# A recurrent layer with a feed-forward beside it: state parts laid out by step, and feed-forward products moved behind the candidate's

## The chip, the core and the metric

The kernel runs on one core of a Trainium2 chip. The metric is the device time of one execution, in microseconds (us). A core has a matrix engine (TensorE, PE in the profile, with its weight loads as PEld), VectorE (DVE), ScalarE (ACT), GpSimd (POOL) and SyncE (SP), each with an instruction stream of its own, and they meet through semaphores.

## What is computed

The first of four layers is a gated recurrent unit over 512 steps for 4 sequences of width 256. A token-wise feed-forward with a hidden width of 1024 follows it, and its output replaces that of the recurrence at selected tokens. Then come a dense layer with experts chosen per sequence, and a layer of 64 experts. Only the first two matter here:

```python
def step(h, xs):
    xzt, xrt, xht = xs
    z = jax.nn.sigmoid(xzt + h @ U_z + vz)
    r = jax.nn.sigmoid(xrt + h @ U_r + vr)
    hh = jnp.tanh(xht + r * h @ U + vh)
    h_new = (1.0 - z) * h + z * hh
    return (h_new, h_new)
...
hidden = jax.nn.gelu(jnp.einsum('bsd,dh->bsh', x, W1) + b1, approximate=False)
blk = jnp.einsum('bsh,hd->bsd', hidden, W2) + b2
```

## The kernel before

**Numbers in parts.** The recurrence multiplies in f16 with every value split in two, a high part and a low part. Each product of a 256-wide vector by a 256x256 matrix is 8 matmuls with the high part of the moving side and 4 with its low part (`recur`). Each has 4 moving columns, one for each sequence.

**One step of the recurrence.** TensorE runs this list for step j, in this order:

1. 12 products of the last step's update (`step_high`, `step_low`) into the reset gate, after which ScalarE takes the tanh of r (L471, `r_h<-bank`);
2. 12 products of the state (shown as `raw`, high then low) into the update gate z, which ScalarE reads at L473 and L474;
3. beside z: one input product for the next window (L772, f32, 160 columns), and in some steps one feed-forward product;
4. 12 products of the gated state (`rh_high`, `rh_low`) into the candidate, whose tanh ScalarE takes at L478 (`z_cand<-bank`);
5. 8 products of the kept part (`keep_part`, high) into the next step's reset gate, then feed-forward products, then the 4 low products of the kept part.

VectorE stands between these. L704 and L595 make the gated state's parts, L711 to L717 the kept part's, L721 and L595 the update's. L730 writes the state's high part into `h16`, L735 and L737 the full state, and L741 the state's low part into `h16`, reading the high part back.

**Windows.** The 512 steps are cut in windows of 40 (`SPAN`), the last of which (12, `FINAL`) has 32. In window w the recurrence runs over its steps. Beside it TensorE makes the input products of window w+1 (36 matmuls, one in each of steps 0 to 35) and the feed-forward of window w-1: 48 up products (L818, 160 moving columns from `h16`) and 48 down products (L833). ScalarE takes the gelu of a hidden tile (L414), VectorE splits it into parts (L660, L663), and ScalarE writes the block's output (L419) and clears its accumulator (L425). GpSimd copies 16 steps of state away at a time (L501).

**What sets the order.** Everything is written out by hand. `up_products` and `down_products` give, for each step jj of a window, which feed-forward products go beside z and which behind the kept part's high products. Steps 0 to 3, 6 to 9, 12 to 15 and 18 to 21 of a window have one up product beside z and two later (16 steps). Steps 16, 17 and 22 to 31 have two down products later, steps 32 to 39 have three. Tuples such as `GELU_AT`, `SPLIT_AT` and `BLOCK_AT` name the steps in which ScalarE and VectorE do their share, always behind the step's own work.

**Layout.** `h16` holds the state's parts as [part, window parity, k and sequence, step]. The 160 columns of an up product are one run. The 4 columns that a recurrent product reads, and the 8 values that L730 and L741 write, stand 40 values (80 bytes) apart.

Of the kernel before, what the change touches and what calls it, by code (L numbers as in the profile page):

```python
# [8 lines left out]
F16 = mybir.dt.float16  # L9
# [31 lines left out]
AHEAD = 2  # L41
EPS = float(np.finfo(np.float32).eps)
# [21 lines left out]
def program(nc, A, out):  # L64
    with ExitStack() as ctx:
# [74 lines left out]
        with ExitStack() as weights:  # L140
# [8 lines left out]
            h16_at, hid16_at, full_at, scale_at = 0, 2 * KD * B * SPAN, 2 * KD * B * SPAN + KH * B * SPAN, 2 * KD * B * SPAN + (KH + 2) * B * SPAN  # L149
            h16 = raw[:, h16_at:hid16_at].bitcast(F16).rearrange("p (x q c t) -> p x q c t", x=2, q=2, c=KD * B)  # L150
            hid16 = raw[:, hid16_at:full_at].bitcast(F16).rearrange("p (x u c) -> p x u c", x=2, u=KH)
            full16 = raw[:, full_at:scale_at].rearrange("p (u c) -> p u c", u=2)
# [3 lines left out]
            under = (w16_1, w16_2, h16, hid16, full16, blk, fsc, silu_c, b1, b2)  # L156
# [6 lines left out]
            last_q = LAST // SPAN % 2  # L163
            last_under = (w16_1, w16_2, lambda x, k: h16[:, x, last_q, k * B:(k + 1) * B, 0:tail],
                          [[hid16[:, x, u, 0:n_last] for u in range(KH)] for x in range(2)],
                          [full16[:, u, 0:n_last] for u in range(2)], blk, fsc, silu_c, b1, b2)
# [41 lines left out]
def gru(nc, sem, A, bank, xT, hist, ident, ones, ones_bf, condT, slot_row, s_x, s_const, load_ffn_up, load_ffn_down, load_next,  # L208
        up_loaded, down_loaded, shared_loaded, raw, shared_parts, under, ffn_sems, wr, wr_rep, idle_rows):

    with ExitStack() as own:
# [3 lines left out]
        w16_1, w16_2, h16, hid16, full16, blk, fsc, silu_c, b1, b2 = under  # L215
# [72 lines left out]
        HIGH_AT, LOW_AT = 3, (7, 8)  # L288
# [42 lines left out]
        FFN_HIGH_AT = ((0, 27), (0, 28), (0, 33), (0, 34), (0, 39), (1, 0), (1, 1), (1, 2))  # L331
# [5 lines left out]
        BLOCK_AT, CLEAR_AT, CLEAR_FINAL_AT = (1, 2), (33, 34), 5  # L337
        GELU_FINAL_AT = (3, 4, 6, 8, 12, 13, 18, 19)
        SPLIT_FINAL_AT = ((4, 5), (6, 7), (8, 9), (10, 11), (13, 14), (15, 16), (19, 20), (21, 22))
        BLOCK_FINAL_AT = (1, 2, 30, 31)  # L340

        def up_products(window, jj):
            if window == FINAL:
                if jj < 6:
                    return 4 * jj, 4 * jj + 2, 4 * jj + 4
                return (2 * jj + 12, 2 * jj + 14, 2 * jj + 14) if jj < 18 else (0, 0, 0)
            at = jj // TERMS * 2 * TERMS + jj % TERMS * 3
            return (at, at + 1, at + 3) if jj < 4 * TERMS and jj % TERMS < 4 else (0, 0, 0)

        def down_products(window, jj):  # L350
            if window == FINAL:
                return (2 * jj - 12, 2 * jj - 10) if 6 <= jj < 30 else (0, 0)
            if jj in (16, 17):
                return 2 * jj - 32, 2 * jj - 30
            if 22 <= jj < 32:
                return 2 * jj - 40, 2 * jj - 38
            return (3 * jj - 72, 3 * jj - 69) if jj >= 32 else (0, 0)

        with nc.Block() as block:
# [20 lines left out]
            def _(act):  # L380
# [27 lines left out]
                def gelu(F):  # L408
                    span, f = F // KH, F % KH
                    n = columns(span)  # L410
                    act.wait_ge(s_fup, F // 2 * 2 + 2)
                    if F >= 2:
                        act.wait_ge(s_flo, F - 1)
                    nc.scalar.activation(full16[:, F % 2, 0:n], up_columns(bank, f, n), ACT.Gelu,  # L414
                                         scale=fsc[:, 9:10], bias=b1[:, f:f + 1]).then_inc(s_gelu, 1)
# [1492 lines left out]
```

## Time and profile before

| what | us |
|---|---|
| median of 3 runs | 2192.7 |
| lowest and highest | 2191.93, 2192.86 |
| the profiled execution | 2195.69 |
| its span, first to last instruction | 2193.8 |
| mean granted TensorE clock | 0.995 of full speed |

The profile lists, for an engine or a line, the busy time, the mean duration of an instruction and what it waited for. A timeline row has the start in us, the busy time of the row, engine, line, operation, output and inputs, the shape and the count, and in brackets the idle time before it with who ended it. The ends of matmuls are modelled, so TensorE's pace is read from the distance between starts. The span falls in two parts: the recurrence with the feed-forward beside it (up to some 1100 us) and all that follows.

### The profile page before, as it was taken

What the parts mean: (1) busy time and instruction counts of PE and PEld (TensorE: products, weight loads), DVE (VectorE), ACT (ScalarE), POOL (GpSimd) and SP (SyncE); (2) the same over time, 40 slices, a digit from 0 to 9 for tenths busy, and PEclk for the clock granted to TensorE, in tenths of its full rate; (3) what the DMA queues carried; (4) which work ended last, traced back from release to release, by engine and by line L of the source; (5) the groups of instructions that cost most, each with busy time, mean ns of one, the idle gap of its engine ahead of it and who ended that gap; (6) DMA issues with size and microseconds to landing.
All of it is one profiled execution on the core that took longest, in us unless ns stands there. A gap on an engine that the chain in (4) does not pass through costs nothing. (4 is left out here: it accounts for less than half of the span.)

```text
span 2193.8 us, 83018 instructions
## 1 busy us (share of the span) xinstructions
PE 2136.1 (97%) x32790; PEld 2007.3 (91%) x32797; DVE 1603.0 (73%) x8952; ACT 1014.6 (46%) x3948; POOL 432.7 (20%) x593
## 2 busy tenths in 40 slices
PE   8999999999999999999979999999999999999997
PEld 7899999999999999999957888866999999999997
DVE  6887777877877877777845555494677777777775
ACT  3555555555555555555545767633222222222221
POOL 0000000000000000000000000254455555555553
PEclk9999999999999999999999999999999999999999
DMA  3001000000000000000000423211888888888882
GB/s 123 4 4 43 4 4 4 4 4 4 4 4 4 4 4 4 4 4 4 4 1 11 153 77 116 104 58 48 297 284 263 285 263 286 265 285 263 282 265 58
DMA packets 55559, 213.74 MB, mean 97 GB/s; under 512 B 11578, under 2 KB 40960, under 8 KB 46976
## 3 DMA queue, kind: packets, MB, share of 16 engines
q1 hardware_dynamic: 36276, 184.41, 22.9%
q0 software_dynamic: 17408, 23.61, 5.7%
q8 instruction: 258, 4.23, 0.8%
q14 instruction: 133, 1.09, 0.2%
q10 hardware_dynamic: 1484, 0.40, 0.1%
HBM read 192.82 MB, written 15.57 MB: 95 GB/s over the span
## 5 line engine op out<-in xcount | busy, mean ns | idle before, releaser
L1789 PE MATMUL bank<-xe,ring 128*128 128x160 f32 x3072 | 439.4, 300 | 0.7 <-DVE xe L1839 0.7
L1789 PEld LDWEIGHTS bank<-xe,ring 128*128 128x128 f32 x3072 | 423.7, 190 | 0.9 <-issue 0.9
L803 PE MATMUL bank<-keep_part,Us 128*128 128x4 f16 x6132 | 322.8, 170 | 0.8 <-DVE keep_part L711 0.4
L803 PEld LDWEIGHTS bank<-keep_part,Us 128*128 128x128 f16 x6132 | 306.1, 111 | 5.0 <-DVE keep_part L717 2.4
L1832 DVE STREAM_TRANSPOSE turned<-ye 32x64 f32<-32x64 f32 x1240 | 291.5, 235 | 16.2
L803 PE MATMUL bank<-raw,Us 128*128 128x4 f16 x6144 | 265.5, 170 | 2.3 <-DVE raw L741 1.7
L1817 ACT ACTIVATE gate_f<-bank 128x160 f32<-128x160 f32 x384 | 116.4, 303 | 288.1 <-PE bank L1789 280.5
L1744 POOL DMA_INDIRECT out_rows<-res,to_row x128 | 192.3, 1503 | 234.7 <-DVE res L1851 201.0
L803 PEld LDWEIGHTS bank<-raw,Us 128*128 128x128 f16 x6144 | 231.8, 104 | 3.0 <-DVE raw L741 2.5
L501 POOL TENSOR_TENSOR hist<-ring,unscale 128x128 f32<-128x128 f32 x32 | 17.0, 531 | 1081.4 <-DVE ring L735 1081.4
L471 ACT ACTIVATE r_h<-bank 128x8 f32<-128x8 f32 x512 | 92.8, 181 | 293.5 <-PE bank L803 293.5
L1798 PE MATMUL bank<-mid,ring 128*128 128x160 f32 x1536 | 220.1, 300 | 2.1 <-DVE mid L1860 2.1
L772 PE MATMUL bank<-in_part,W_part 128*128 128x160 f32 (+1 forms) x468 | 215.0, 474 | 0.0
L1798 PEld LDWEIGHTS bank<-mid,ring 128*128 128x128 f32 x1536 | 212.7, 190 | 2.4 <-DVE mid L1860 2.4
L803 PE MATMUL bank<-rh_high,Us 128*128 128x4 f16 x4096 | 205.9, 172 | 8.3 <-DVE rh_high L704 0.5
L1860 DVE TENSOR_TENSOR mid<-bank,gate_f 128x160 f32<-128x160 f32 x384 | 117.5, 317 | 130.8 <-ACT gate_f L1817 120.7
L803 PEld LDWEIGHTS bank<-rh_high,Us 128*128 128x128 f16 x4096 | 183.7, 113 | 24.2 <-DVE rh_high L704 18.3
L803 PE MATMUL bank<-step_high,Us 128*128 128x4 f16 x4096 | 190.2, 168 | 6.1 <-issue 0.8
L476 ACT ACTIVATE z_cand<-tz,lift 128x8 f32<-128x8 f32 x512 | 156.0, 305 | 16.5
L803 PEld LDWEIGHTS bank<-step_high,Us 128*128 128x128 f16 x4096 | 149.2, 105 | 14.3 <-DVE step_high L721 3.6
L721 DVE TENSOR_TENSOR step_high<-z_cand 128x8 f16<-128x8 f32 x512 | 89.4, 175 | 96.4 <-ACT z_cand L478 83.3
L818 PE MATMUL bank<-raw,ffn_parts 128*128 128x160 f16 x576 | 148.4, 330 | 0.0
(269 smaller groups left out, 4088.4 us busy)
## 6 DMA issues: line engine op xcount, KB each, us to landing
ring<-in_ew SPq DMA_DIRECT2D x64, 2304.0 KB
raw<-in_L_cond_ew SPq DMA_DIRECT2D x16, 1024.0 KB, 6.3
ctx_rows<-rows SPq DMA_DIRECT2D x2, 1280.0 KB, 6.7
dense_w<-in_L_ffn_W SPq DMA_DIRECT2D x2, 1024.0 KB, 9.4
dense_w<-in_L_cond_sw SPq DMA_DIRECT2D x2, 1024.0 KB, 6.3
out_rows<-orow SPq DMA_DIRECT2D x4, 512.0 KB, 3.9
out_rows<-res,to_row POOLq DMA_INDIRECT x128
xT<-in_xT SPq DMA_DIRECT2D x2, 864.0 KB, 10.4
```

Of the source, the lines that this page charges most:

```text
L471: nc.scalar.activation(r, pre_of(0, q, jj), ACT.Tanh, scale=inv[0]).then_inc(s_r, 1)
L476: nc.scalar.activation(z, tz[:], ACT.Identity, scale=2.0 ** (STATE_EXP - 1), bias=lift[:, 0:1]).then_inc(s_z, 1)
L721: nc.vector.tensor_tensor(step_high[:, :, 2], z, cand, ALU.mult).then_inc(s_shi, 1)
L772: last = nc.tensor.matmul(product(span, n), W_part[w][:, g, k, m * P:(m + 1) * P], steps_of(x_part[x], span)[:, k], start=(k == 0 and i == ...
L803: last = nc.tensor.matmul(pre[g][q][:, jj, m, :], Us[:, g, p, k, m * P:(m + 1) * P], x[part][:, k * B:(k + 1) * B], start=False, stop=Fals ...
L818: last = nc.tensor.matmul(up_columns(bank, f, columns(span)), w16_1[w][:, k, f * P:(f + 1) * P], h16[:, x, span % 2, k * B:(k + 1) * B, 0: ...
L1744: nc.gpsimd.indirect_dma_start(out=out[:, :], out_offset=bass.IndirectOffsetOnAxis(ap=to_idx[c][:, 0:1], axis=0), in_=res[e % 2][c][:], in ...
L1789: last = nc.tensor.matmul(bank[f % UPS][:, s_ * CAP:(s_ + 1) * CAP], w1[u][:, k, s_ * FFN + f * P:s_ * FFN + (f + 1) * P], xe[e % 2][:, k] ...
L1798: last = nc.tensor.matmul(bank[6 + e % 2][:, d * CAP:(d + 1) * CAP], w2[u][:, f, d * P:(d + 1) * P], mid[e % 2][:, f], start=(f == 0), sto ...
L1817: nc.scalar.activation(gate[:, f % 2], bank[f % UPS][:, CAP:2 * CAP], ACT.Silu).then_inc(s_silu, 1)
L1832: last = nc.vector.transpose(y[:, :, q, :], ye[e % 2][q * SQ:(q + 1) * SQ, :, j * SQ:(j + 1) * SQ])
L1860: nc.vector.tensor_tensor(mid[e % 2][:, f], bank[f % UPS][:, 0:CAP], gate[:, f % 2], ALU.mult).then_inc(s_mid, 1)
```

## The change

The layout: `h16` becomes `h_steps`, [part, window parity, step, k and sequence]. The 8 values of one step are one run, so L730 and L741 write one run and a recurrent product reads 4 adjacent values. The 160 columns of an up product are now 40 runs of 4 values (8 bytes) that start 16 bytes apart. The hidden tile's columns are therefore ordered by step and then sequence, and the block's output is read from the accumulator with a step of 4 values.

The order: no feed-forward product stands beside z, except in the final window. All come right behind the candidate's products and ahead of all of the kept part's.

```diff
-            h16 = raw[:, h16_at:hid16_at].bitcast(F16).rearrange("p (x q c t) -> p x q c t", x=2, q=2, c=KD * B)
+            h_steps = raw[:, steps_at:hid16_at].bitcast(F16).rearrange("p (x q t c) -> p x q t c", x=2, q=2, t=SPAN)
...
-        HIGH_AT, LOW_AT = 3, (7, 8)
+        HIGH_AT, LOW_AT = 4, (7, 8)
...
-        def h16_of(p, j):
+        def part_of(p, j):
             if j < 0:
-                return h16[:, p, 1, :, SPAN - 1]
-            return h16[:, p, j // SPAN % 2, :, j % SPAN]
+                return h_steps[:, p, 1, SPAN - 1]
+            return h_steps[:, p, j // SPAN % 2, j % SPAN]
...
-        SHARED_HIGH_AT = [(span, at) for span in range(3, 7) for at in (0, 4)]
-        SHARED_LOW_AT = [(span, at) for span in range(3, 7) for at in (1, 2, 3, 4, 5, 6, 9, 14)]
+        SHARED_HIGH_AT = [(span, SPAN - 1) for span in range(3, 11)]
+        SHARED_LOW_AT = [(span, at) for span in range(4, 12) for at in range(LOWS)]
...
+        UP = count([(0, 3, 3, 3, 3, 0)[jj] if jj < TERMS else (3, 3, 2, 2, 2, 0)[jj % TERMS] if jj < 4 * TERMS else 0 for jj in range(SPAN)])
+        DOWN = count([3 if jj in (17, 23) or 24 <= jj < 34 else 2 if jj >= 34 else 0 for jj in range(SPAN)])
+        UP_FINAL_BESIDE_Z = count([2 if 1 <= jj <= 16 else 0 for jj in range(TAIL)])
+        UP_FINAL_LATER = count([1 if 1 <= jj <= 16 else 0 for jj in range(TAIL)])
+        DOWN_FINAL_BESIDE_Z = count([2 if 17 <= jj < 24 else 0 for jj in range(TAIL)])
+        DOWN_FINAL_LATER = count([2 if 8 <= jj < 25 else 0 for jj in range(TAIL)])
...
-                                         block_columns(bank, span, d, columns(span)).rearrange("p (b t) -> p b t", b=B),
+                                         block_columns(bank, span, d, columns(span)).rearrange("p (t b) -> p b t", b=B),
...
-                                            h16[:, x, span % 2, k * B:(k + 1) * B, 0:LENGTHS[span]],
+                                            h_steps[:, x, span % 2, 0:LENGTHS[span], k * B:(k + 1) * B],
...
+                        if span:
+                            for n in later[0]:
+                                ffn_up(span, n)
+                            if later[1] and span < FINAL:
+                                pe.wait_ge(s_tz, m)
+                            for n in later[1]:
+                                ffn_down(span, n)
                         nq, njj = (q, jj + 1) if jj < LENGTHS[span] - 1 else (1 - q, 0)
                         if m < S:
                             if njj == 0:
                                 pe.wait_ge(s_seed, (span + 1) * GROUPS * B)
                             pe.wait_ge(s_khi, m)
                             recur(0, nq, njj, kept, 0)
-                        if span:
-                            for n in range(middle, end):
-                                ffn_up(span, n)
-                            if down_products(span, jj)[1]:
-                                pe.wait_ge(s_z, m)
-                            for n in range(*down_products(span, jj)):
-                                ffn_down(span, n)
-                        if m < S:
                             pe.wait_ge(s_klo, m)
                             recur(0, nq, njj, kept, 1)
```

The gelu's output gets 8 buffers in place of 2 (`FULLS`). The steps of some ScalarE and VectorE work shift: the block's output from steps 1 and 2 to 2 and 3, the split of the shared expert's weights (L687 and its high half) from windows 3 to 6 to the last and first four steps of windows 3 to 11, and those of the final window. The up products no longer wait for the seeding of the next window; the input products wait for the gelu that frees their bank from tile 2 on.

TensorE in step 6 of window 2, before, from the input product to the end of the step; `raw,ffn_parts` are feed-forward products:

```order
L772 MATMUL bank<-in_part,W_part 128x160
L818 MATMUL bank<-raw,ffn_parts 128x160 [waits ffn_hidden_done]
L803 MATMUL bank<-rh_high,Us 128x4 [waits rh_hi]
L803 MATMUL bank<-rh_high,Us 128x4 x7
L803 MATMUL bank<-rh_low,Us 128x4 [waits rh_lo]
L803 MATMUL bank<-rh_low,Us 128x4 x3
L803 MATMUL bank<-keep_part,Us 128x4 [waits keep_hi]
L803 MATMUL bank<-keep_part,Us 128x4 x7
L818 MATMUL bank<-raw,ffn_parts 128x160 x2
L803 MATMUL bank<-keep_part,Us 128x4 [waits keep_lo]
L803 MATMUL bank<-keep_part,Us 128x4 x3
```

The same place in the changed kernel:

```order
L784 MATMUL bank<-in_part,W_part 128x160
L815 MATMUL bank<-rh_high,Us 128x4 [waits rh_hi]
L815 MATMUL bank<-rh_high,Us 128x4 x7
L815 MATMUL bank<-rh_low,Us 128x4 [waits rh_lo]
L815 MATMUL bank<-rh_low,Us 128x4 x3
L828 MATMUL bank<-raw,ffn_parts 128x160 [waits ffn_hidden_done]
L828 MATMUL bank<-raw,ffn_parts 128x160 x2
L815 MATMUL bank<-keep_part,Us 128x4 [waits keep_hi]
L815 MATMUL bank<-keep_part,Us 128x4 x7
L815 MATMUL bank<-keep_part,Us 128x4 [waits keep_lo]
L815 MATMUL bank<-keep_part,Us 128x4 x3
```

The up product that stood ahead of the candidate's products now stands behind them with the two others, and the three stand ahead of the kept part's high products.

TensorE in step 24 of window 2, before, behind the gated state's low products:

```order
L803 MATMUL bank<-keep_part,Us 128x4 [waits keep_hi]
L803 MATMUL bank<-keep_part,Us 128x4 x7
L833 MATMUL bank<-raw,ffn_parts 128x160 [waits z_done]
L833 MATMUL bank<-raw,ffn_parts 128x160
L803 MATMUL bank<-keep_part,Us 128x4 [waits keep_lo]
L803 MATMUL bank<-keep_part,Us 128x4 x3
```

The same place in the changed kernel:

```order
L843 MATMUL bank<-raw,ffn_parts 128x160 [waits ffn_hidden_low,z_turned]
L843 MATMUL bank<-raw,ffn_parts 128x160 x2
L815 MATMUL bank<-keep_part,Us 128x4 [waits keep_hi]
L815 MATMUL bank<-keep_part,Us 128x4 x7
L815 MATMUL bank<-keep_part,Us 128x4 [waits keep_lo]
L815 MATMUL bank<-keep_part,Us 128x4 x3
```

Three down products stand there in place of two, ahead of the kept part's high products, and they wait for the tanh of z (L474) and no longer for z itself (L476).

## Rows read from the trace of the kernel before

**Rows 1.** Busy time of each engine in window 7: us, busy (instructions), clock, DMA.

```profile
core 0: us, PE busy (x) PEld busy (x) DVE busy (x) ACT busy (x) POOL busy (x), PEclk, DMA share, GB/s
614.20:698.20 84.00, 83.16 (x2056) 81.61 (x2054) 65.75 (x498) 46.88 (x237) 1.15 (x3) 1.00 0.02 4
```

**Rows 2.** ScalarE's timeline: tanh of r opening windows 7, 8, 12; second row step 1.

```profile
614.20 0.18 ACT L471 ACTIVATE r_h<-bank 128x8 f32<-128x8 f32 x1 [0.90 <-PE bank L803]
...
616.31 0.18 ACT L471 ACTIVATE r_h<-bank 128x8 f32<-128x8 f32 x1 [0.81 <-PE bank L803]
...
698.25 0.18 ACT L471 ACTIVATE r_h<-bank 128x8 f32<-128x8 f32 x1 [0.90 <-PE bank L803]
...
1035.65 0.18 ACT L471 ACTIVATE r_h<-bank 128x8 f32<-128x8 f32 x1 [0.90 <-PE bank L803]
```

**Rows 3.** Timeline of window 7, step 12 (one up product beside z).

```profile
639.76 0.18 ACT L471 ACTIVATE r_h<-bank 128x8 f32<-128x8 f32 x1 [0.57 <-PE bank L803]
...
639.96 0.48 PE L772 MATMUL bank<-in_part,W_part 128*128 128x160 f32 x1
...
640.25 0.36 PE L818 MATMUL bank<-raw,ffn_parts 128*128 128x160 f16 x1
...
640.39 0.40 PE L803 MATMUL bank<-rh_high,Us 128*128 128x4 f16 x8
...
640.94 0.18 ACT L478 ACTIVATE z_cand<-bank 128x8 f32<-128x8 f32 x1 [0.21 <-PE bank L803]
...
641.93 0.18 ACT L471 ACTIVATE r_h<-bank 128x8 f32<-128x8 f32 x1 [0.57 <-PE bank L803]
```

**Rows 4.** Timeline of window 7, step 26 (input product alone beside z).

```profile
669.59 0.18 ACT L471 ACTIVATE r_h<-bank 128x8 f32<-128x8 f32 x1 [0.57 <-PE bank L803]
...
669.80 0.48 PE L772 MATMUL bank<-in_part,W_part 128*128 128x160 f32 x1
...
670.08 0.42 PE L803 MATMUL bank<-rh_high,Us 128*128 128x4 f16 x8
...
670.64 0.18 ACT L478 ACTIVATE z_cand<-bank 128x8 f32<-128x8 f32 x1
...
671.46 0.20 DVE L741 SCALAR_TENSOR_TENSOR raw<-ring,raw 128x8 f16<-128x8 f32 x1
671.63 0.18 ACT L471 ACTIVATE r_h<-bank 128x8 f32<-128x8 f32 x1 [0.57 <-PE bank L803]
...
671.84 0.48 PE L772 MATMUL bank<-in_part,W_part 128*128 128x160 f32 x1
```

**Rows 5.** Timeline of window 12, step 5 (two up products, no input product).

```profile
1045.76 0.18 ACT L471 ACTIVATE r_h<-bank 128x8 f32<-128x8 f32 x1 [0.44 <-PE bank L803]
...
1045.96 0.43 PE L818 MATMUL bank<-raw,ffn_parts 128*128 128x160 f16 x2
...
1046.20 0.38 PE L803 MATMUL bank<-rh_high,Us 128*128 128x4 f16 x8
...
1047.74 0.18 ACT L471 ACTIVATE r_h<-bank 128x8 f32<-128x8 f32 x1 [0.39 <-PE bank L803]
```

**Rows 6.** Timeline of window 7, steps 32 and 33 (three down products later).

```profile
681.86 0.18 ACT L471 ACTIVATE r_h<-bank 128x8 f32<-128x8 f32 x1 [0.59 <-PE bank L803]
...
683.95 0.18 ACT L471 ACTIVATE r_h<-bank 128x8 f32<-128x8 f32 x1 [0.61 <-PE bank L803]
...
685.99 0.18 ACT L471 ACTIVATE r_h<-bank 128x8 f32<-128x8 f32 x1 [0.66 <-PE bank L803]
```

**Rows 7.** Two VectorE lines: duration of one, ns, min/median/max.

```profile
L741 DVE SCALAR_TENSOR_TENSOR raw<-ring,raw x512: 193/195/233, 24.3 to 1100.1; 128x8 f16<-128x8 f32 x171
...
L717 DVE TENSOR_TENSOR keep_part<-keep,keep_part x512: 166/167/169, 23.3 to 1099.4; 128x8 f16<-128x8 f32 x171
```

**Rows 8.** Groups of instructions by line and shape: busy us, mean ns, idle before.

```profile
L1044 PE MATMUL bank<-x_part,weights_part 128*128 128x512 f32 x576 | 136.8, 395 | 5.4 <-DVE x_part L1229 5.4
...
L419 ACT ACTIVATE ffn_out<-bank,b,raw 128x160 f32<-128x160 f32 x24 | 11.5, 478 | 0.0
```

More of the change, by code:

```diff
@@ L41 @@
 AHEAD = 2
+FULLS = 8
 EPS = float(np.finfo(np.float32).eps)
@@ L339, in gru @@
[L339 to L357, printed above, removed]
+        BLOCK_AT, CLEAR_AT = (2, 3), (33, 34)
+        GELU_FINAL_AT = (5, 6, 9, 10, 13, 14, 17, 18)
+        SPLIT_FINAL_AT = ((6, 7), (8, 9), (10, 11), (12, 13), (14, 15), (16, 17), (18, 19), (20, 21))
@@ new lines, in gru, with count @@
+        BLOCK_FINAL_AT, CLEAR_FINAL_AT, BLOCK_LAST_AT = (2, 3), (4, 7), (26, 27)
+        def count(steps):
+            at = [0]
+            for n in steps:
+                at.append(at[-1] + n)
+            return at
+        UP_TERMS = [(k, w, 0) for k in range(KD) for w in range(2)] + [(k, 0, 1) for k in range(KD)]
+        TAIL = LENGTHS[FINAL]
+        NONE = [0] * (SPAN + 1)
+        UP = count([(0, 3, 3, 3, 3, 0)[jj] if jj < TERMS else (3, 3, 2, 2, 2, 0)[jj % TERMS] if jj < 4 * TERMS else 0 for jj in range(SPAN)])
@@ new lines, in gru, with ffn_products @@
+        DOWN = count([3 if jj in (17, 23) or 24 <= jj < 34 else 2 if jj >= 34 else 0 for jj in range(SPAN)])
[3 more added lines that the diff above has]
+        DOWN_FINAL_LATER = count([2 if 8 <= jj < 25 else 0 for jj in range(TAIL)])
+        def ffn_products(window, jj):
+            up_a, up_b = (UP_FINAL_BESIDE_Z, UP_FINAL_LATER) if window == FINAL else (NONE, UP)
+            down_a, down_b = (DOWN_FINAL_BESIDE_Z, DOWN_FINAL_LATER) if window == FINAL else (NONE, DOWN)
+            assert up_a[-1] + up_b[-1] == down_a[-1] + down_b[-1] == KH * TERMS
+            at = [v[jj] + w[jj] for v, w in ((up_a, up_b), (down_a, down_b))]
+            mid = [at[0] + up_a[jj + 1] - up_a[jj], at[1] + down_a[jj + 1] - down_a[jj]]
+            end = [mid[0] + up_b[jj + 1] - up_b[jj], mid[1] + down_b[jj + 1] - down_b[jj]]
+            return ([range(at[x], mid[x]) for x in range(2)], [range(mid[x], end[x]) for x in range(2)])
@@ L430, in ffn_scalar @@
                             gelu((window - 1) * KH + GELU_FINAL_AT.index(jj))
-                        if jj in BLOCK_FINAL_AT:
-                            at = BLOCK_FINAL_AT.index(jj)
-                            block_out(window - 2 + at // KD, at % KD)
-                        if jj == CLEAR_FINAL_AT:
-                            for d in range(KD):
+                        for d in range(KD):
+                            if jj == BLOCK_FINAL_AT[d]:
+                                block_out(window - 2, d)
+                            if jj == CLEAR_FINAL_AT[d]:
                                 block_clear(window - 2, d)
+                            if jj == BLOCK_LAST_AT[d]:
+                                block_out(window - 1, d)
                     else:
@@ L439, in ffn_scalar @@
                             gelu((window - 1) * KH + GELU_AT.index(jj))
-                        if window >= 2 and jj in BLOCK_AT:
-                            block_out(window - 2, BLOCK_AT.index(jj))
-                        if window >= 2 and jj in CLEAR_AT:
-                            block_clear(window - 2, CLEAR_AT.index(jj))
+                        for d in range(KD):
+                            if window >= 2 and jj == BLOCK_AT[d]:
+                                block_out(window - 2, d)
+                            if window >= 2 and jj == CLEAR_AT[d]:
+                                block_clear(window - 2, d)
                     if (window, jj) in FFN_HIGH_AT:
@@ L729, in _ @@
                         dve.wait_ge(s_fup, (span - 1) * KH)
-                    nc.vector.scalar_tensor_tensor(out=h16_of(0, j), in0=step_in[:], scalar=2.0, in1=keep[:],
+                    nc.vector.scalar_tensor_tensor(out=part_of(0, j), in0=step_in[:], scalar=2.0, in1=keep[:],
                                                    op0=ALU.mult, op1=ALU.add).then_inc(s_hhi, 1)
@@ L813, in ffn_up @@
                             pe.wait_ge(s_gelu, span * KH + f - 2)
-                        if f >= 4 and window < FINAL:
-                            pe.wait_ge(s_seed, (window * GROUPS + f // 2 - 1) * B)
                         if span == 0:
@@ L861, in _ @@
                         recur(0, q, jj, step, 1).then_inc(s_rp, 1)
-                        state = [h16_of(p, STARTS[span] + jj - 1) for p in range(2)]
+                        state = [part_of(p, STARTS[span] + jj - 1) for p in range(2)]
                         pe.wait_ge(s_hhi, m)
@@ L866, in _ @@
                         recur(1, q, jj, state, 1).then_inc(s_zp, 1)
+                        beside_z, later = ffn_products(span, jj)
                         if jj < len(ahead):
@@ L870, in _ @@
                             ahead[jj]()
-                        first, middle, end = up_products(span, jj)
                         if span:
-                            for n in range(first, middle):
+                            for n in beside_z[0]:
                                 ffn_up(span, n)
+                            for n in beside_z[1]:
+                                ffn_down(span, n)
                         pe.wait_ge(s_rhhi, m)
```

46 lines of the change are left out of this document (23 added, 23 removed).

## The prediction, made before the changed kernel had run

> **What bounds the kernel now.** I first looked at the busy times by stretch. Within a window TensorE is busy for 83.16 of 84.00 us [rows 1], but its modelled ends cover short gaps, so the share does not tell whether work or waiting sets the pace. That is read from ScalarE's tanh of r, which opens each step: the distance between two of them is a step's length. Window 7 lasts 698.25 - 614.20 = 84.05 us for 40 steps [rows 2]. Next I compared steps of different content.
>
> A step with one input product and one up product beside z takes 641.93 - 639.76 = 2.17 us [rows 3]. One with the input product alone takes 671.63 - 669.59 = 2.04 [rows 4]. One with two up products beside z and no input product takes 1047.74 - 1045.76 = 1.98 [rows 5]. The first two classes give 16 x 2.17 + 24 x 2.04 = 83.7, so they account for nearly all of the window.
>
> The reader should see where the 0.13 sits. From the tanh of r to the candidate's first product it is 0.63 in the slow step (640.39 - 639.76), 0.49 in the middle one (670.08 - 669.59) and 0.44 in the last (1046.20 - 1045.76). The gated state is ready at about 0.44, since there the products start as VectorE delivers. In the slow step TensorE is still busy: the input product starts at +0.20 and takes until +0.49, and the up product holds it for another 640.39 - 640.25 = 0.14. From the candidate's tanh to the next tanh of r it is 641.93 - 640.94 = 0.99 in the slow step, which has two up products later, and 671.63 - 670.64 = 0.99 in the middle one, which has two down products later. So two later products fit within the wait for the candidate, and a product beside z behind an input product does not.
>
> **The change part by part.**
>
> *The up product leaves z's side.* In windows 1 to 11 this makes 16 steps like the middle one. Fifteen of them save 2.17 - 2.04 = 0.13, which is 1.95 a window. The step that opens a window takes 2.11 (616.31 - 614.20) [rows 2] and saves 0.07. Together it is 2.02, and 22.2 us in 11 windows. Some of these steps are held by something else as well (the copying of the state by GpSimd, and in window 1 the double splits of weights on VectorE), where the up product is partly hidden. I take a tenth off by choice: **-20 us**.
>
> *It returns later.* In ten steps of a window there are now three later ups, in twelve three later downs, in the rest two or none. Steps 32 and 33 of window 7 already have an input product and three later downs. The first takes 683.95 - 681.86 = 2.09, since TensorE comes late to the update's products; the second takes 685.99 - 683.95 = 2.04 [rows 6], since its own lateness is matched by the earlier input product. So a run of such steps costs 0.05 once, part of which comes back at its end. Five runs a window, less the one there is now, and 0.01 to 0.05 each: **+1 us**, at most +2.
>
> *Downs thinned at the end.* Steps 36 to 39 have no input product and now two downs for three. Their length lies between 2.04 [rows 6] and the 1.98 of rows 5, and two products without an input product give 1.98. I take 0.05 for 4 x 11 steps: **-2 us**, between 0 and -2.6.
>
> *The low part of the state.* L741 takes 195 ns. L717 also reads one f32 and one f16 operand of 8 values and writes 8 f16, all adjacent, and takes 167 [rows 7]. With adjacent values I expect L741 to become like it, 28 ns less. This is on the path: in the middle step L741 starts at 671.46 and ends 0.20 later, and the input product at 671.84 is 0.18 behind that end, time enough for a semaphore and four low products. The input product then starts 0.03 earlier, and so do the candidate's products, which it holds back by 0.05. It applies in steps with an input product and not over two later products: 14 a window in 11 windows and 36 in window 0, 190 in all, or 5.3 us. Between 0 and -5.3 I take **-4 us**, as the step behind a run of three has this already.
>
> *The runs of four.* No row of the kernel shows a matmul that streams 160 columns in runs of four f16 values, 16 bytes from start to start. The nearest is the f32 operand of L1044, where four columns also take 16 bytes: at most 136.8 / 576 = 0.24 us for 512 columns [rows 8], 0.47 ns a column. At that pace 160 columns take 0.07 us, under the 0.14 that an up product holds TensorE today. I take 0, and keep as the other end a doubling of the 0.14 (a rival below). A gain is excluded for the up products, since their operand was one run before.
>
> The Trainium skill, Advanced Engine Details and Errata, section Memory Cachelines, says that SBUF is read in 16-byte lines, that at least two hits on a line are needed for full speed, and that a new line for each access costs. Four columns fall in each line here, so by it the ups lose nothing. The same rule speaks for a gain in the recurrence, whose state columns stood 80 bytes apart; the rows read here do not separate such a cost, so only a run can tell. By the rule the sum would be some us lower.
>
> *Covered work.* The block's output (L419, 478 ns [rows 8]) is now read with a step of four values. It runs behind the candidate's tanh, which in the middle step is followed by 0.99 us before ScalarE is needed; 0.18 of tanh and 0.48 leave 0.33. Only beyond 0.8 us would it delay a step, and then two steps a window. The shared weights' splits, now in steps with no up product beside z, sit on VectorE behind L741 as the hidden tile's splits do in front of the middle step, which is 2.04 all the same. The new wait for the tanh of z has the candidate's products ahead of it, which end later; queued behind it are the kept part's products.
>
> *The final window.* Nine of its steps now have two ups beside z and three products later, where two and two fitted in 1.98. By rows 6 a late third costs up to 0.05: **+0.5 us**. The tail after the recurrence has 48 matmuls on the new layout, and I count nothing.
>
> Sum: -20 + 1 - 2 - 4 + 0.5 = -24.5, call it -25. Against the profiled execution of 2195.69 that is 2170.7. The median of the runs is 3.0 lower than it, so the forecast is **2167.7 us**. About 0.2% (4.4 us) is what a measurement of this kernel can tell from no change.
>
> **The rivals.**
>
> *Partly given back, 2180 us.* Either each step with three later products costs 0.05 and not only the first of a run (22 x 11 x 0.05 = 12 us), or the runs of four add some 20 ns to each of 528 up products (11 us). For it speaks that such steps have no slack [rows 6]; against it the 2.04 of step 33.
>
> *More than forecast, 2158 us.* The 28 ns show in nearly all steps, and the recurrent products also gain some ns each from adjacent columns. 440 + 36 steps at 0.02 more are 10 us.
>
> *Nothing gained, 2193 us.* The candidate's products start earlier but the path runs elsewhere, through the kept part, which now stands behind the feed-forward products. Against it: four of the kept part's twelve products stood behind the feed-forward products before as well, and in the step of rows 4 that still gave 0.99 us from the candidate's tanh to the next tanh of r; TensorE's work between the two is the same in sum.
>
> *Slower: the stream of the ups.* If short runs slow the stream, all 48 ups of a window sit in places without slack. The cost is 528 x per up, less 5 us for the little slack of steps with two. The point from which it decides is (25 + 5) / 528 = 0.057 us an up, that is 0.20 in place of 0.14. Doubled, it is 528 x 0.14 - 5 = 69 us, and the kernel takes 2237 us. For it speaks only that no row shows this pattern; against it the pace of L1044.
>
> **How the numbers follow.** Forecast 0.64, partly given back 0.18, more 0.08, nothing 0.05, slower 0.05. The forecast and the gain beyond it are faster, and most of the partial case is: faster 0.88, same 0.06, slower 0.06. The range of 2156 to 2183 takes in the low ends of the terms (22.2 + 2.6 + 5.3 = 30 us of gain), some of the case of more, and the partial case, and leaves out the last two and a little more.
>
> **What would show it.** Steps 0 to 21 of a window at 2.01 to 2.05 us where 2.17 stood, with the candidate's products 0.46 to 0.49 behind the tanh of r. L741 at 165 to 170 ns. Steps 1 to 4 equal in length to steps 24 to 33; if they are longer, the stream of the ups is slower than that of the downs. Windows of some 81.8 us. All after the recurrence unchanged. I am wrong if steps 1 to 4 exceed 2.1 us, or if the candidate's products start at 0.49 and the step is still 2.1 or more.

## The result: 2155.0 us for 2192.3, and the profile after

| | before | after |
|---|---|---|
| median of 4 runs, us | 2192.31 | 2155.03 |
| lowest and highest | 2191.37, 2192.86 | 2153.85, 2156.48 |
| span of the profiled execution | 2193.8 | 2154.0 |
| mean granted TensorE clock | 0.995 | 0.995 |

The ratio is 0.9831, with a 95% interval from 0.9814 to 0.9848. The kernel gained 37 us where 25 were forecast, and the time lies 1 us below the range of 2156 to 2183.

First the busy times of window 7 of the changed kernel (us, then busy time and instructions of each engine), which answer to [rows 1]:

```profile
594.79:675.92 81.13, 80.32 (x2058) 78.37 (x2056) 64.04 (x502) 47.34 (x238) 1.18 (x3) 1.00 0.01 4
```

The window takes 81.13 us in place of 84.05, though TensorE and the others have the same instructions to do, but for a few at the edges and the shifted splits. ScalarE's timeline at the starts of windows 7, 8 and 12 and at the last step, as in [rows 2]:

```profile
594.79 0.18 ACT L483 ACTIVATE r_h<-bank 128x8 f32<-128x8 f32 x1 [0.30 <-PE bank L815]
...
675.92 0.18 ACT L483 ACTIVATE r_h<-bank 128x8 f32<-128x8 f32 x1 [0.30 <-PE bank L815]
...
1000.81 0.18 ACT L483 ACTIVATE r_h<-bank 128x8 f32<-128x8 f32 x1 [0.81 <-PE bank L815]
...
1063.33 0.18 ACT L483 ACTIVATE r_h<-bank 128x8 f32<-128x8 f32 x1 [0.81 <-PE bank L815]
```

The first step starts at 22.48 in both. The last one starts at 1063.33 and started at 1098.14 before, so 34.8 of the 39.8 us between the two spans lie in the recurrence. The rest is taken up at the end of the experiments.

Step 12 of window 7, the slow step of [rows 3], now with three up products later:

```profile
619.16 0.18 ACT L483 ACTIVATE r_h<-bank 128x8 f32<-128x8 f32 x1 [0.57 <-PE bank L815]
...
619.32 0.48 PE L784 MATMUL bank<-in_part,W_part 128*128 128x160 f32 x1
...
619.61 0.41 PE L815 MATMUL bank<-rh_high,Us 128*128 128x4 f16 x8
...
619.98 0.56 PE L828 MATMUL bank<-raw,ffn_parts 128*128 128x160 f16 x3
...
620.34 0.50 PE L815 MATMUL bank<-keep_part,Us 128*128 128x4 f16 x12
...
621.20 0.18 ACT L483 ACTIVATE r_h<-bank 128x8 f32<-128x8 f32 x1 [0.61 <-PE bank L815]
```

It takes 2.04 us and took 2.17. From the tanh of r the candidate's products start at +0.45, as early as in the step of [rows 5] that has no input product at all. Three ups take 620.34 - 619.98 = 0.36. Step 9 of the same window has two ups later:

```profile
612.73 0.14 DVE L742 SCALAR_TENSOR_TENSOR raw<-step_in,keep 128x8 f16<-128x8 f32 x1
612.79 0.16 DVE L747 SCALAR_TENSOR_TENSOR ring<-keep,step_in 128x8 f32<-128x8 f32 x1
...
612.98 0.17 DVE L753 SCALAR_TENSOR_TENSOR raw<-ring,raw 128x8 f16<-128x8 f32 x1
...
613.18 0.18 ACT L483 ACTIVATE r_h<-bank 128x8 f32<-128x8 f32 x1 [0.57 <-PE bank L815]
...
613.34 0.48 PE L784 MATMUL bank<-in_part,W_part 128*128 128x160 f32 x1
...
613.62 0.41 PE L815 MATMUL bank<-rh_high,Us 128*128 128x4 f16 x8
...
615.17 0.18 ACT L483 ACTIVATE r_h<-bank 128x8 f32<-128x8 f32 x1 [0.43 <-PE bank L815]
```

It takes 1.99 us. I had expected 2.01 or 2.02. The input product starts at +0.16, where it started at +0.21 in [rows 4]. That is 0.05 earlier, not the 0.03 of the forecast. VectorE's two writes of the state's parts show why (ns of one, min/median/max). The first is the changed kernel's L742, which was L730:

```profile
L742 DVE SCALAR_TENSOR_TENSOR raw<-step_in,keep x512: 139/141/168, 24.0 to 1065.0; 128x8 f16<-128x8 f32 x171
L753 DVE SCALAR_TENSOR_TENSOR raw<-ring,raw x512: 166/167/171, 24.3 to 1065.3; 128x8 f16<-128x8 f32 x171
```

And the same write of the high part in the kernel before, which the prediction had no row of:

```profile
L730 DVE SCALAR_TENSOR_TENSOR raw<-step_in,keep x512: 165/167/193, 24.0 to 1099.9; 128x8 f16<-128x8 f32 x171
```

L741 went from 195 to 167 as forecast. L730 went from 167 to 141, which was not priced. How much of the 26 ns reaches the low part's write is seen from where that write starts. Ahead of L741 in the kernel before, at 671.46 in [rows 4]:

```profile
671.19 0.17 DVE L730 SCALAR_TENSOR_TENSOR raw<-step_in,keep 128x8 f16<-128x8 f32 x1
671.24 0.16 DVE L735 SCALAR_TENSOR_TENSOR ring<-keep,step_in 128x8 f32<-128x8 f32 x1
```

The low part's write reads the full state (L735, now L747) and the high part, and the kernel makes it wait for both. Before, it started 271 ns behind the start of the high part's write, and now it starts 252 ns behind it (medians of the 512 steps). So some 20 of the 26 ns come through. In 50 steps of windows 2 to 11 (steps 5, 11, 15, 34 and 35) it started 102 to 104 ns behind the end of the high part's write before, and 51 to 59 behind that of the full state's. Now it starts 109 to 114 behind the first and 33 to 35 behind the second. The distance that hardly varies tells what it waits for: the high part's write before, and, with that one shortened, the full state's write now.

### The profile page after: what moved, and what is told of

It is laid out like the page before. It is cut to its first block and busy times, and to the rows that moved or that the text cites. A ratio compares the mean times of both kernels' runs of the same rounds, so it can differ in the third digit from the quotient of the medians.

```text
span 2154.0 us, 83007 instructions
## 1 busy us (share of the span) xinstructions
PE 2100.0 (97%) x32790; PEld 1966.0 (91%) x32797; DVE 1570.9 (73%) x8952; ACT 1014.5 (47%) x3948; POOL 432.2 (20%) x593
## 5 line engine op out<-in xcount | busy, mean ns | idle before, releaser
L815 PEld LDWEIGHTS bank<-keep_part,Us 128*128 128x128 f16 x6132 | 274.0, 111 | 2.2 <-DVE keep_part L729 0.4
L815 PE MATMUL bank<-keep_part,Us 128*128 128x4 f16 x6132 | 262.1, 170 | 0.4 <-DVE keep_part L729 0.3
L1828 ACT ACTIVATE gate_f<-bank 128x160 f32<-128x160 f32 x384 | 116.4, 303 | 283.1 <-PE bank L1800 282.2
L815 PE MATMUL bank<-raw,Us 128*128 128x4 f16 x6144 | 240.1, 167 | 2.0 <-issue 1.2
L513 POOL TENSOR_TENSOR hist<-ring,unscale 128x128 f32<-128x128 f32 x32 | 16.5, 514 | 1047.0 <-DVE ring L747 1047.0
L815 PEld LDWEIGHTS bank<-raw,Us 128*128 128x128 f16 x6144 | 208.1, 105 | 2.4 <-issue 1.3
L815 PEld LDWEIGHTS bank<-rh_high,Us 128*128 128x128 f16 x4096 | 160.5, 111 | 34.7 <-DVE rh_high L716 24.4
L1055 PE MATMUL bank<-x_part,weights_part 128*128 128x512 f32 x576 | 137.1, 396 | 5.4 <-DVE x_part L1240 5.4
```

The source lines that it names most:

```text
L815: last = nc.tensor.matmul(pre[g][q][:, jj, m, :], Us[:, g, p, k, m * P:(m + 1) * P], x[part][:, k * B:(k + 1) * B], start=False, stop=Fals ...
L1055: last = nc.tensor.matmul(up[f % len(up)][:], w[i][:, k, f * P:(f + 1) * P], x[j][:, k], start=(k == 0 and i == 0 and j == 0), stop=(k == ...
L1828: nc.scalar.activation(gate[:, f % 2], bank[f % UPS][:, CAP:2 * CAP], ACT.Silu).then_inc(s_silu, 1)
```

## The experiments

The theory after the result (A) has two links. VectorE writes the high part, and the write of the low part waits for it; TensorE's four low products wait for that one, and the input product and the candidate's products stand behind them. Adjacent values make both writes shorter, by 26 and 28 ns, of which 20 and 28 reach TensorE. A lightly loaded (light) step is one with an input product, nothing else beside z and at most two later products. The rival (B) is the forecast's own account: one link of 28 ns, in lightly loaded steps, with the order bringing nearly everything. Each kernel was timed in 3 rounds beside the kernel before.

### The layout alone

```diff
-h16 = raw[...].rearrange("p (x q c t) -> p x q c t", ...)
+h16 = raw[...].rearrange("p (x q t c) -> p x q t c", ...)
```

All other lines that read or write `h16` follow. The order is that of the kernel before.

> The kernel before with the state's parts laid out by step and the up products streaming runs of four, and with the order of all products as before. Theory A (two links): VectorE's write of the high part takes 26 ns less and its write of the low part 28 ns less, and both lie in a row on the way to the input product, so steps with an input product and nothing else beside z go from 2.04 to 1.99 us, slow steps from 2.17 to 2.12, window 0 loses 1.4 us, steps 32 to 35 stay: some 2173 us. Theory B (one link, as forecast): only the low part's 28 ns count, and only in lightly loaded steps: 2187 us or more.

Measured: 2175.68 us (2173.08 to 2176.84), ratio 0.9919 [0.9902, 0.9935]. The tanh of r at steps 2 and 3, then at 26 and 27 of window 7:

```profile
609.27 0.18 ACT L471 ACTIVATE r_h<-bank 128x8 f32<-128x8 f32 x1 [0.44 <-PE bank L803]
611.40 0.18 ACT L471 ACTIVATE r_h<-bank 128x8 f32<-128x8 f32 x1 [0.44 <-PE bank L803]
...
659.32 0.18 ACT L471 ACTIVATE r_h<-bank 128x8 f32<-128x8 f32 x1 [0.57 <-PE bank L803]
661.31 0.18 ACT L471 ACTIVATE r_h<-bank 128x8 f32<-128x8 f32 x1 [0.57 <-PE bank L803]
```

A slow step takes 2.13, one with the input product alone 1.99. From the first to the last tanh of r it is 1058.4 us for 1075.7. The layout by itself brings 17 us, as theory A has it, and three times the 5.3 that were my upper bound.

### The order alone

```diff
-h_steps = raw[...].rearrange("p (x q t c) -> p x q t c", ...)
+h_steps = raw[...].rearrange("p (x q c t) -> p x q c t", ...)
```

This is the changed kernel with the old layout.

> The changed kernel with the old layout of the state's parts (the four columns of a step 80 bytes apart, the up products one run of 160). Theory A: steps with an input product and at most two later products take 2.04 us, those with three later 2.04 to 2.05, window 0 as before (84.6 us): 2168 to 2171 us, so the order brings some 22 to 24 us and the two parts overlap in the steps with three later products. Theory B: the order brings nearly all of it, 2160 us or less.

Measured: 2168.39 us (2168.01 to 2168.71), ratio 0.9889 [0.9873, 0.9906]. The two writes, and step 9 of window 7:

```profile
L742 DVE SCALAR_TENSOR_TENSOR raw<-step_in,keep x512: 166/169/197, 24.5 to 1077.6; 128x8 f16<-128x8 f32 x171
L753 DVE SCALAR_TENSOR_TENSOR raw<-ring,raw x512: 193/196/202, 24.8 to 1077.9; 128x8 f16<-128x8 f32 x171
...
620.99 0.18 ACT L483 ACTIVATE r_h<-bank 128x8 f32<-128x8 f32 x1 [0.57 <-PE bank L815]
...
621.20 0.48 PE L784 MATMUL bank<-in_part,W_part 128*128 128x160 f32 x1
...
623.03 0.18 ACT L483 ACTIVATE r_h<-bank 128x8 f32<-128x8 f32 x1 [0.43 <-PE bank L815]
```

The input product is back at +0.21 and the step at 2.04. From the first to the last tanh of r it is 1053.0 us, 22.7 less than before. The recurrence gains 17.3 by the layout, 22.7 by the order and 34.8 by both, so 5 us overlap. They are lost in the steps with three later products, where earlier state parts bring less. With the order alone the first step of a run of them takes 2.09 and the others 2.05 (medians over windows 2 to 11); in the changed kernel they take 2.04 and 2.03.

### One part of the state in the old layout

The changed kernel, once with the low part and once with the high part kept 80 bytes apart:

```diff
+h_high, h_low = h_steps[:, 0], <h_steps[:, 1] with the values of a step 80 bytes apart>
```

> The changed kernel with the high part by step and the low part in the old layout, 80 bytes apart. If each link counts by itself, the high part's write takes 141 ns as in the changed kernel and the low part's between 167 and 195; steps without later products (0, 5, 11) then take 1.99 plus what the low part's write takes over 167, up to 2.02. A third of the up products stream values 80 bytes apart: if short runs slow a stream, steps 1 to 4 grow beyond 2.04, by 3 x 1/3 of the cost of one. 2155 to 2165 us.

> The changed kernel with the low part by step and the high part in the old layout, 80 bytes apart: the mirror of the run with the low part apart. Theory A (what costs is writing 8 f16 values apart, not reading them): the high part's write takes 167 ns again, the low part's, which reads the high part 80 bytes apart but writes one run, 167 too, and the lightly loaded steps are 2.02, as there. Theory C (reading apart costs): the low part's write takes about 195. Two thirds of the up products stream values 80 bytes apart; at the 0.14 to 0.15 us that each cost in the two runs before, 352 of them give 50 us: some 2205 us.

Measured: 2180.86 us (2179.49 to 2181.15) with the low part apart, 2202.86 (2202.50 to 2203.52) with the high part apart. The writes with the low part apart (L743, L754), then with the high part apart:

```profile
L743 DVE SCALAR_TENSOR_TENSOR raw<-step_in,keep x512: 140/142/169, 24.1 to 1089.0; 128x8 f16<-128x8 f32 x171
L754 DVE SCALAR_TENSOR_TENSOR raw<-ring,raw x512: 192/195/199, 24.4 to 1089.2; 128x8 f16<-128x8 f32 x171
```

```profile
L743 DVE SCALAR_TENSOR_TENSOR raw<-step_in,keep x512: 166/168/195, 23.6 to 1111.6; 128x8 f16<-128x8 f32 x171
L754 DVE SCALAR_TENSOR_TENSOR raw<-ring,raw x512: 170/172/176, 23.9 to 1111.9; 128x8 f16<-128x8 f32 x171
```

Whoever writes the values apart pays 26 to 28 ns; reading the high part apart costs the low part's write 5 ns (172 for 167). The two links are separate and each counts: step 35, with an input product and two downs, takes 2.02 (the median over windows 2 to 11) in either kernel, against 1.99 with both parts by step and 2.04 with neither (order alone). Steps 25 to 30, with three downs, need only one of the two: 2.03 in either kernel and with both, 2.05 with neither.

These runs also show what TensorE gains from reading four adjacent values, which is nothing. The eight high products of the state are 187 ns from the first start to the last with the high part 80 bytes apart, and 186 with it by step (medians, light steps). The four low products are 81 ns from first to last with the low part apart, and 80 with the high part apart.

Most of the time lost in these two kernels is another matter, the up products' stream. The changed kernel makes each hidden tile from four ups of the high part and then two of the low part. With the low part apart, a step whose three ups include two of the low part takes 2.29. With the high part apart, one with three of the high part takes 2.45 to 2.49 and one with a single one 2.17. The changed kernel has 2.03 to 2.04 there.

### How finely the up products' operand may be cut

The changed kernel with the columns of an up product in another order, so that they are read in runs of one or of two values, always 16 bytes from run to run:

```diff
+h_steps[:, x, span % 2, 0:LENGTHS[span], k * B:(k + 1) * B].rearrange("p t c -> p c t")
...
+h_steps[:, x, span % 2, 0:LENGTHS[span], k * B:(k + 1) * B].rearrange("p t (h w) -> p h t w", w=2)
```

> The changed kernel with the up products' columns ordered by sequence and then step, so that each of the 160 columns starts 16 bytes from the one before (runs of one in place of four). If the stream does not mind, 2155 us and steps 1 to 4 at 2.04. If a new 16 bytes for each column halves the pace of 160 columns at 0.47 ns (0.07 us), each up costs 0.07 more: steps 1 to 4 at 2.2, 2190 us or more.

> The changed kernel with the up products' columns in runs of two f16 values (4 bytes), runs 16 bytes apart. Runs of four cost nothing and runs of one 0.15 us a product. If the pace is one 16-byte line in a fixed time, 160 columns in runs of two take half as long as in runs of one and hide in part: steps 1 to 4 at some 2.1 to 2.2 us, 2165 to 2195 us. If two values in a line are enough, 2155 us as with four.

Measured: 2233.34 us (2232.41 to 2233.93) in runs of one, 2158.33 (2156.43 to 2160.24) in runs of two. Three ups and the kept part's products behind them in window 7, in runs of one and then of two:

```profile
640.89 1.01 PE L828 MATMUL bank<-raw,ffn_parts 128*128 128x160 f16 x3
641.72 0.48 PE L815 MATMUL bank<-keep_part,Us 128*128 128x4 f16 x12
```

```profile
621.96 0.59 PE L828 MATMUL bank<-raw,ffn_parts 128*128 128x160 f16 x3
...
622.38 0.48 PE L815 MATMUL bank<-keep_part,Us 128*128 128x4 f16 x12
```

From the first of three ups to the kept part's products it is 0.83 us in runs of one, 0.42 in runs of two and 0.36 in runs of four. Steps 1 to 4 of the changed kernel (three ups) and steps 24 to 31 (three downs, whose operand is one run) are both 2.03 to 2.04 us, so the operand in runs of four is all but free: three ups take 359 ns in the changed kernel and 353 with the order alone, whose operand is one run (medians). In runs of two it costs 0.02 us a product more than in runs of four, in runs of one 0.16. I had expected 0.07 for runs of one (steps 1 to 4 at 2.2, where 2.49 came). For runs of two my expectation left both answers open, and half the cost of one was too high.

The slower rival of the prediction named this mechanism. By its formula 0.157 us more for each up product gives 528 x 0.157 - 5 = 78 us over the changed kernel, and 2233.3 - 2155.0 = 78.3 came out. That the two agree so closely is luck. In windows 1 to 11, which the 528 products are, the traces differ by 67.3 us, since a step with two ups hides 0.10 of its 0.31 and grows from 1.99 to 2.20. The final window, which the formula leaves out, adds 4.7, and 5.0 lie behind the recurrence. The mechanism is real, and the rival's price, 0.14 more for each up, was near the 0.157; it starts at runs shorter than those of this change.

### Where the later products stand, and what a product beside z costs

The later products between the kept part's high and low products, as before the change; and one of each step's ups back beside z:

```diff
-(feed-forward products), recur(kept, high), recur(kept, low)
+recur(kept, high), (feed-forward products), recur(kept, low)
```

```diff
+UP_BESIDE_Z = count([1 if b > a else 0 for a, b in zip(UP, UP[1:])])
+UP_LATER = count([b - a - 1 if b > a else 0 for a, b in zip(UP, UP[1:])])
```

> The changed kernel with the later feed-forward products between the kept part's high and low products, where they stood before. TensorE's work between the candidate's products and the update's is the same in sum, so the place should not matter: 2155 us, steps unchanged at 1.99 and 2.04. If the kept part's place matters (its high products waiting for VectorE when nothing is ahead of them), the lightly loaded steps differ.

> The changed kernel with one up product back beside z in each of the 19 steps that have ups. The input product ends at +0.44, as the gated state is ready, so the up product delays the candidate by its own 0.13 to 0.14: these steps take 2.12, against 2.04 in ten and 1.99 in nine of them, 2.0 us a window, 2177 us. If an earlier input product leaves room for it, less.

Measured: 2157.41 us (2154.73 to 2158.84) with the products behind the kept part's high ones, and from the first to the last tanh of r 1040.9 us, as in the changed kernel. Their place among the kept part's products does not matter. With one up beside z: 2177.37 (2176.12 to 2178.66), as expected. Its step 2 in window 7:

```profile
610.80 0.18 ACT L485 ACTIVATE r_h<-bank 128x8 f32<-128x8 f32 x1 [0.81 <-PE bank L817]
...
611.25 0.36 PE L830 MATMUL bank<-raw,ffn_parts 128*128 128x160 f16 x1
...
611.40 0.40 PE L817 MATMUL bank<-rh_high,Us 128*128 128x4 f16 x8
...
612.93 0.18 ACT L485 ACTIVATE r_h<-bank 128x8 f32<-128x8 f32 x1 [0.44 <-PE bank L817]
```

The up product holds back the candidate's products by 0.15, to +0.60, and the step takes 2.13. Steps with three ups grow by 0.08 to 0.10, steps with two by 0.14.

### One more operation ahead of the low part

```diff
+nc.vector.scalar_tensor_tensor(out=spare[:], in0=keep[:], scalar=0.5, in1=step_in[:],
+                               op0=ALU.mult, op1=ALU.add)
 dve.wait_ge(s_h, m + 1)
```

> The changed kernel with one more VectorE operation on 8 values (its result not used) ahead of the low part's write, about 0.08 us. Theory A (the low part is on the path to the input product): steps with an input product and at most two later products go from 1.99 to 2.05, window 0 grows by some 2 us, steps with three later products by 0.03 at most, steps 36 to 39 not at all: about 2172 us. Theory B (it was the adjacent columns in TensorE's recurrent products that gained): no change, 2155 us.

Measured: 2162.08 us (2159.56 to 2162.55), 7 us more than the changed kernel, less than half of the 17 expected. Step 9 of window 7, with the added operation (L752), the low part's write (L756) and the input product:

```profile
618.59 0.16 DVE L752 SCALAR_TENSOR_TENSOR spare<-keep,step_in 128x8 f32<-128x8 f32 x1
618.67 0.16 DVE L756 SCALAR_TENSOR_TENSOR raw<-ring,raw 128x8 f16<-128x8 f32 x1
...
618.82 0.18 ACT L484 ACTIVATE r_h<-bank 128x8 f32<-128x8 f32 x1 [0.57 <-PE bank L818]
...
619.01 0.48 PE L787 MATMUL bank<-in_part,W_part 128*128 128x160 f32 x1
```

The low part's write starts 618.82 - 618.67 = 0.15 before the tanh of r and started 613.18 - 612.98 = 0.20 before it. Unrounded it is 158 ns for 195 (medians of light steps), so it is 0.04 late and not 0.08. In the changed kernel VectorE had been waiting there for its own earlier writes to arrive, and the added operation fills some of that wait. It is also 8 ns shorter (159 for 167, the medians). The input product starts at +0.19 for +0.16, and a light step takes 2.03. The theory holds: a later low part costs. Steps with three later products stay at 2.03, except the first of each run, which grows from 2.04 to 2.07. My size for the delay did not take the wait into account.

### Fewer buffers, and fewer steps with three later products

```diff
-FULLS = 8
+FULLS = 2
```

> The changed kernel with 2 buffers for the gelu's output in place of 8. The gelu of a tile then waits for the split two tiles before, which comes six steps earlier, so nothing waits: 2155 us and the same steps. If the buffers carried part of the gain, some steps grow.

Measured: 2155.68 us (2154.96 to 2156.86). The buffers have no part in the gain.

```diff
-UP = count([(0, 3, 3, 3, 3, 0)[jj] if jj < TERMS else ...
+UP = count([(3, 3, 2, 2, 2, 0)[jj] if jj < TERMS else ...
...
+DOWN_BESIDE_Z = count([{36: 2, 37: 2, 38: 1}.get(jj, 0) for jj in range(SPAN)])
```

> The changed kernel with fewer steps of three later products, 16 for 22: the first run of ups is 3, 3, 2, 2, 2 like the others, and five down products of the last two tiles go beside z in steps 36 to 38, where no input product is (behind a wait for r). If a step with three later products costs 0.045 more than one with two, a window loses 6 x 0.045 = 0.27 us, 3 us in all: 2152 us. If the products beside z in steps 36 to 38 delay the candidate, nothing or less.

Measured: 2154.29 us (2151.88 to 2155.17), which can't be told from the changed kernel's 2155.03. Windows 2 to 11 take 810.9 us for 812.2, so 0.13 a window came in place of 0.27. Steps 2 to 4, 17, 23, 32 and 33 do fall, from 2.03 or 2.04 to 1.99 or 2.00. But the step that opens a window, which now has three ups, grows from 1.99 to 2.04, and steps 36 and 37 from 1.99 to 2.01.

### What lies behind the recurrence

From the last tanh of r to the end it was 1095.7 us before and is 1090.7 in the changed kernel, and the change touches little there. The experts' stage differs, seen from its first to its last gated tile (L1817, then L1828 after):

```profile
L1817 ACT ACTIVATE gate_f<-bank x384: 303/303/304, 1534.8 to 2174.8; 128x160 f32<-128x160 f32 x192
```

```profile
L1828 ACT ACTIVATE gate_f<-bank x384: 303/303/304, 1500.2 to 2136.1; 128x160 f32<-128x160 f32 x192
```

It takes 640.0 and 635.9 us. In the kernel before, the list of waits has one idle time of ScalarE there for which no engine of the core stands:

```profile
ACT gate_f L1817 <- remote: 2.6, 1, 2.6
```

The kernels with the layout alone, the order alone, the low part apart and runs of one have one such wait of 5.5 us each, in front of another instruction, and a stage of 636.7 to 637.0. The changed kernel and the other seven experiments have none among their longest waits. What it is, and why some programs have it, stays open. The stage accounts for 4.1 of the 39.8 us between the two profiled spans, and no reason above rests on it.

## Why the prediction was wrong

*What bounds the kernel, and the up product beside z.* Right. The slow step had its 0.13 where the prediction put it, between the tanh of r and the candidate's products, and it went. In the changed kernel too, one back beside z delays the candidate by 0.15.

*The order in all.* The terms on it were -20, +1, -2 and +0.5. The order alone gave -22.7 in the recurrence. The tenth that I took off by choice was about the miss, though step 8 of every other window does stay at 2.19 in the changed kernel. In step 8 of window 7 VectorE's work on the inputs (L534) meets GpSimd's copying (L513) and takes 0.66 us, where it takes 0.32 in windows 6 and 8:

```profile
610.80 0.52 POOL L513 TENSOR_TENSOR hist<-ring,unscale 128x128 f32<-128x128 f32 x1 [32.01 <-DVE ring L747]
...
610.84 0.66 DVE L534 TENSOR_TENSOR in_part<-xT,in_part 128x160 fp32r<-128x160 f32 x1
```

The edge of a window gave more than said: its last step went from 2.07 to 1.99 by the order alone. With the order alone three later products cost as said, some 0.05 once a run (2.09, then 2.05 for the 2.04 of a light step). In the changed kernel each of the 22 steps costs 0.04 over a light one, because the layout shortened the light ones to 1.99.

*The low part of the state: the step that failed.* The prediction put -4 us on it, at most -5.3. On top of the order the layout gives 1053.0 - 1040.9 = 12.1 us in the recurrence, and 2168.4 - 2155.0 = 13.4 us in the whole. Two things were wrong in it. The term took only L741's 28 ns, and L730, whose 8 values went just as far apart into the same tile, had to shorten too (167 to 141 ns). And the chain was cut one link short: what starts L741 is the end of L730, so 20 of the 26 ns pass through, until the full state's write takes over. With 48 ns in place of 28 the input product starts 0.05 earlier (204 to 156 ns behind the tanh of r), the candidate's products reach the 0.44 of a step without an input product, and the light steps are at 1.99 in place of 2.04. From the order alone to the changed kernel the light steps gain 0.50 us a window and window 0 gains 1.5, 7 us in all.

The steps with three later products gain too, 5 us in all, where the prediction had nothing: 0.05 in the first step of a run, 0.01 to 0.02 in the others. This is the state's parts again and not TensorE reading adjacent values. Steps 25 to 30 reach the same 2.03 with the high part or the low part still 80 bytes apart, and the state's products take as long with a part apart as with it adjacent. I had looked at the instruction whose wait is visible to TensorE, and not at the one that it waits for.

*The runs of four.* Right: 2 ns a product, as good as no cost, as the pace of L1044 suggested. The Trainium skill's rule (Advanced Engine Details and Errata, Memory Cachelines: at least two hits on a 16-byte line absorb the access latency, a new line for each access is penalised) agrees with the three widths measured. Three ups take 0.83 us with one value per 16 bytes, 0.42 with two and 0.36 with four. The gain that the prediction read from the same rule for the recurrence's products does not show: 187 ns apart, 186 adjacent for eight of them.

*Covered work and the final window.* The block's output, now read with a step of four values, takes the 478 ns of [rows 8] again and hides:

```profile
L429 ACT ACTIVATE ffn_out<-bank,b,raw x24: 478/478/479, 193.7 to 1056.5; 128x160 f32<-128x160 f32 x24
```

Window 12 takes 62.52 us from its first to its last tanh of r, and took 62.49; +0.5 was put.

*The rivals.* "More than forecast" (2158) came closest. It had 28 ns in nearly all steps and some ns from TensorE's reads; the writes gave 48 in the light steps and the reads nothing. "Partly given back" was right that each step with three later products costs, 0.04 and not only in the first of a run, but only against light steps that had gained 0.05. "Nothing gained" had no part. The slower one needed runs shorter than four.

*The range.* Its low end added the low ends of terms of which one had its bound from a single instruction. With L730 in it, that bound would have been nearly twice as wide and the range would have held the time. Whether the time fell just inside or just outside the range was in part chance: the 34.8 us of the recurrence alone would give 2192.3 - 34.8 = 2157.5, inside the range, and the rest of the gain lies behind the recurrence, where the cause stays open and the prediction had said unchanged.

## What to carry to other kernels

When a layout changes, list every instruction that writes or reads the tile, take the duration of each, and follow the chain of waits backwards from the one that you price: a write that ends earlier also starts the next one earlier, until another wait takes over. Keep the 8 or so values that VectorE writes in a small, latency-bound operation in one run. An f16 operand of TensorE can be streamed in runs of four (8 bytes in every 16) for nothing, and in runs of one it costs 0.16 us more for 160 columns. A long matmul in front of a waiting chain costs its whole length once the work ahead of it already fills the gap, and much less behind the chain's own products (two of them fitted in here, a third cost 0.04 us a step).

## What the runs showed that was not expected

- VectorE pays 26 to 28 ns more for writing 8 f16 values 80 bytes apart than for one run (167 for 141, 195 for 167), and 5 ns for reading one f16 operand apart (172 for 167).
- 160 f16 columns streamed in runs of one value, 16 bytes from start to start, hold TensorE 0.28 us each in a row of three; in runs of two 0.14; in runs of four 0.12, as for a single run of 160.
- Four f16 columns that TensorE reads 80 bytes apart cost it nothing over four adjacent ones: eight such products are 187 ns from first to last start, and 186.
- Two gains of 17.3 and 22.7 us in the same chain give 34.8 together, since the steps with three later products gain little from the second.
